# Second layer norm to first attention pair, reordered: token sums taken from PSUM, one gate chain for all tiles, odd value units and the first head's weights ahead of the experts

## What is computed

```
xn = layernorm(x)
x  = x + s4_convolution(xn) + swiglu_ffn(xn)
xn = layernorm(x)
x  = x + attention(xn) + lora_moe(xn)
```

## Time and profile before

| | |
|---|---|
| median of 3 runs | 1158.82 us (1155.83, 1158.82, 1159.38) |
| the profiled execution's own time | 1157.67 us |
| its span | 1155.8 us |
| TensorE busy | 1116.6 us, 97% of the span |
| VectorE, ScalarE, GpSimd busy | 680.5, 443.9, 741.8 us (59%, 38%, 64%) |
| TensorE's granted clock, mean | 0.988 of full speed |

### The profile page before, as it was taken

One profiled execution on the slowest core, in us unless ns is written; L12 is line 12 of the kernel. 1 busy time (PEld: TensorE's weight loads), 2 busy tenths in 40 slices (PEclk: granted clock), 3 DMA queues, 4 the chain that ended last, 5 costly groups with the idle time before them and its releaser, 6 DMA issues.

```text
span 1155.8 us, 19611 instructions
## 1 busy us (share of the span) xinstructions
PE 1116.6 (97%) x5822; PEld 956.6 (83%) x5822; DVE 680.5 (59%) x1673; ACT 443.9 (38%) x1287; POOL 741.8 (64%) x1107
## 2 busy tenths in 40 slices
PE   7989999986999999999999999999999999999997
PEld 7768888886788888888888888888888888888886
DVE  5777256287546546645664565466547645654575
ACT  2221132121344434444444444344434443444452
POOL 3654487767358766775876587667757766775552
PEclk8999999988999999999999999999999999999999
DMA  6212432111001101110111011002101110111001
GB/s 209 91 60 69 138 100 73 55 60 56 18 20 65 46 20 54 39 37 18 54 36 36 27 64 46 26 22 69 36 18 54 36 36 18 54 37 55 11 10 73
DMA packets 24825, 59.12 MB, mean 51 GB/s; under 512 B 3536, under 2 KB 3856, under 8 KB 24656
## 3 DMA queue, kind: packets, MB, share of 16 engines
q1 hardware_dynamic: 24784, 58.61, 15.5%
HBM read 56.50 MB, written 2.10 MB: 51 GB/s over the span
## 4 chain that ended last, share of the span: by engine, by line
PE 87%; DVE 7%; issue 2%; ACT 2%; POOL 1%; DMA 0%; SPq 0%; POOLq 0%; DVEq 0%; ACTq 0%
PE banks L169 26%; PE banks L171 26%; PE banks L170 26%; PE banks L1447 4%; PE banks L1438 2%; PE banks L1463 2%; DVE banks L1251 1%; POOL prob L1187 0%; PE banks L812 0%; ACT prob L1346 0%; DVE mixed L553 0%; ACT kT_hi L1229 0%; DMA acc<-in_x 0%; DVE prob L1368 0%; ACT oT_hi L1355 0%
## 5 line engine op out<-in xcount | busy, mean ns | idle before, releaser
L1186 POOL TENSOR_SCALAR prob<-prob,inv 128x128 f32<-128x128 f32 x128 | 48.0, 375 | 258.2 <-DVE inv L1374 258.2
L1159 POOL TENSOR_TENSOR form_lo<-wqk_stage,form_hi 128x256 fp32r<-128x256 f32 x192 | 142.0, 739 | 16.0
L1387 DVE TENSOR_TENSOR acc<-acc,banks 128x512 f32<-128x512 f32 x128 | 87.6, 685 | 81.1 <-PE banks L171 79.9
L1346 ACT ACTIVATE prob<-prob,top 128x128 f32<-128x128 f32 (+1 forms) x256 | 114.9, 452 | 34.9 <-DVE top L1368 34.5
L169 PE MATMUL banks<-tT_hi,form_hi 128*128 128x512 f32 x256 | 105.3, 411 | 0.0
L1368 DVE CUSTOM_DVE_ANT_0 prob<-banks,mask 128x128 f32<-128x128 f32 (+1 forms) x256 | 80.7, 353 | 40.2 <-PE banks L171 40.1
L171 PE MATMUL banks<-tT_hi,form_lo 128*128 128x512 f32 x256 | 100.2, 391 | 0.0
L169 PE MATMUL banks<-wv_hi,xT_hi 128*128 128x512 f32 x256 | 99.9, 390 | 0.0
L170 PE MATMUL banks<-tT_lo,form_hi 128*128 128x512 f32 x256 | 99.8, 390 | 0.0
L171 PE MATMUL banks<-wv_hi,xT_lo 128*128 128x512 f32 x256 | 99.6, 389 | 0.0
L170 PE MATMUL banks<-wv_lo,xT_hi 128*128 128x512 f32 x256 | 99.6, 389 | 0.0
(11 more groups left out here) (263 smaller groups left out, 3127.7 us busy)
## 6 DMA issues: line engine op xcount, KB each, us to landing
wqk_stage<-in_w_qk SPq DMA_DIRECT2D x32, 512.0 KB, 3.2
gu_stage<-in_w_gu SPq DMA_DIRECT2D x22, 512.0 KB, 3.3
wvo_stage<-in_w_v SPq DMA_DIRECT2D x32, 256.0 KB, 3.5
wvo_stage<-in_w_o SPq DMA_DIRECT2D x32, 256.0 KB, 2.6
wd_stage<-in_w_down SPq DMA_DIRECT2D x22, 256.0 KB, 2.6
acc<-in_x SPq DMA_DIRECT2D x8, 256.0 KB, 5.1
out<-acc SPq DMA_DIRECT2D x8, 256.0 KB, 2.0
tab<-in_w_comb SPq DMA_DIRECT2D x1, 1300.0 KB, 6.5
```

Source lines behind the costliest of these rows:

```text
L1159: nc.gpsimd.tensor_tensor(form_lo[:, part], src[:, :], as_f32(form_hi[:, part]), ALU.subtract).then_inc(form_ready, 1)
L1186: nc.gpsimd.tensor_scalar(prob[:, i, 0:P], prob[:, i, 0:P], inv[:, i, 0:1], 1.0, ALU.mult, ALU.mult)
L1346: ins = nc.scalar.activation(pr, pr, ACT.Exp, bias=top[:, n % 2, r:r + 1], scale=-1.0, accum_out=total[:, n % 2, r:r + 1])
L1387: nc.vector.tensor_tensor(acc[:, t, :], acc[:, t, :], turn_bank(steps, step), ALU.add).then_inc(w_added, 1)
```

## The change

The change edits only order, buffers and the way some sums are formed:

- **Token sums.** ScalarE copies only the first halves of the banks (256 of 512 columns) of tiles 0 to 3 and, new, those of tiles 4 to 7 (`b1`). A new VectorE step `keep(t)` takes one difference while tiles 0 to 3 are transposed. `mix(t)` becomes three instructions: two of 256 columns with one operand in PSUM and one of 512 columns with both in SBUF. Before it had two with a PSUM operand and two with none, of 256 columns each. The features of `tT` stand in another order, and P4 is combined with a subtraction.
- **Gates.** One chain for all eight tiles, behind `linear_add(7)`; the exponential's table is loaded ahead by a small activation behind `hg_copy(3)`. `hg`, `hw`, `ge`, `gw` and `gt` hold all tiles.
- **Value units 1, 3, 5, 7** of group 0 go ahead of P1, P6 and the gated transposes; the rest of head 0's ahead steps are spread finer. The first five slots lose these units.
- **GpSimd** makes all seven forms of head 0 between its two blocks of bias adds, behind a wait on the last down projection, and splits the four value pieces between `tT_lo` of tile 1 and of tile 2. The first two query and key loads wait for the last gate and up products and no longer for the end of the convolution; for this `wqk_stage` and the `late` buffers lie elsewhere.
- **Experts** use two banks (5 and 7) and no longer three; the wait for the last expert add moves to S of pair 1.
- In `OUTER_SLOTS` unit `("W", 1, 5)` and product `("P", 3, P4)` change places, and in the last group the pieces `WO[2:4]` are split at pair 13 and no longer at pair 14.

```diff
+AHEAD_V = 1, 3, 5, 7
 FIRST_SLOTS = [
-    [("L", 0, P5), ("V", 0), ("Y", 0), ("V", 1), ("P", 0, P3), ("P", 1, P1)],
-    [("L", 0, P3), ("P", 1, P6), ("V", 2), ("Y", 2), ("P", 1, P2), ("V", 3)],
-    [("L", 1, P2), ("P", 1, P7), ("V", 4), ("Y", 4), ("P", 1, P4), ("V", 5)],
-    [("L", 1, P4), ("P", 1, P5), ("V", 6), ("Y", 6)],
-    [("L", 1, P5), ("V", 7), ("P", 1, P3)]]
+    [("L", 0, P5), ("V", 0), ("Y", 0), ("P", 0, P3)],
+    [("L", 0, P3), ("V", 2), ("P", 1, P1), ("Y", 2), ("P", 1, P6)],
+    [("P", 1, P2), ("L", 1, P2), ("P", 1, P7), ("P", 1, P4)],
+    [("L", 1, P4), ("V", 4), ("Y", 4), ("P", 1, P5)],
+    [("L", 1, P5), ("V", 6), ("Y", 6), ("P", 1, P3)]]
...
-LAST_SPLITS = [[task for task in slot if task[0] != "wv" and (task[0] == "wo" or task[1] < GH)] for slot in SPLITS]
+LAST_SPLITS = [[task for task in slot if task[0] not in ("wv", "wo") and task[1] < GH] for slot in SPLITS]
+LAST_SPLITS[5], LAST_SPLITS[13] = WO[0:2], WO[2:4]
...
     def expert_bank(n):
-        return D + 1 + n % 3
+        return D + 1 + 2 * (n % 2)
...
             if t == TH:
+                pool.wait_ge(wd_used, 2 * NF)
                 ahead(0)
...
         for t in range(TH):
+            if t == 2:
+                ahead(1)
...
-        ahead(1)
...
         for t in range(TH):
             act.wait_ge(xT_done, NT + t + 1)
-            nc.scalar.activation(xh[:, t, :], banks[:, G + t, :], ACT.Copy).then_inc(xh_done, 1)
+            nc.scalar.activation(xh[:, t, 2 * P:], banks[:, G + t, 0:2 * P], ACT.Copy)
             xT_evac(NT + t, G + t)
         sqrt_var(4)
         hg_copy(range(0, 2))
-        for t in range(TH, NT):
-            xT_evac(NT + t, D + t - TH)
-        for t in range(2):
+        for t in range(TH):
+            act.wait_ge(xT_done, NT + TH + t + 1)
+            nc.scalar.activation(b1[:, t, :], banks[:, D + t, 0:2 * P], ACT.Copy)
+            xT_evac(NT + TH + t, D + t)
+        for t in range(TH):
             mixed_evac(t)
-        hg_copy(range(2, 3))
-        for t in range(2, TH):
-            mixed_evac(t)
-        hg_copy(range(3, TH))
-        gate_exps(0)
+            if t % 2:
+                hg_copy(range(2 + t // 2, 3 + t // 2))
+        nc.scalar.activation(gt[:, 9, :], gt[:, 8, :], ACT.Exp)
         hg_copy(range(TH, NT))
-        gate_exps(1)
+        gate_exps()
         ahead(0)
         hwT_evac(0)
+        ahead(1)
         hwT_evac(1)
-        ahead(1)
+        ahead(2)
...
+        def keep(t):
+
+            nc.vector.tensor_tensor(xh[:, t, 0:2 * P], xh[:, t, 2 * P:], banks[:, G + t, 2 * P:],
+                                    ALU.subtract).then_inc(x_kept, 1)
...
-            link(nc.vector.tensor_tensor(t1, b1, a1, ALU.subtract))
-            link(nc.vector.tensor_tensor(t2, b2, t1, ALU.subtract))
-            nc.vector.tensor_tensor(t3, t2, a1, ALU.subtract)
-            nc.vector.tensor_tensor(t4, a2, t2, ALU.subtract).then_inc(x_mixed, 1)
+            nc.vector.tensor_tensor(t1, wide(banks[:, D + t, 0:2 * P], 2), wide(xh[:, t, 2 * P:], 2), ALU.subtract)
+            link(nc.vector.tensor_tensor(t3, wide(banks[:, D + t, 2 * P:], 2), wide(b1[:, t, :], 2), ALU.subtract))
+            dve.wait_ge(x_kept, t + 1)
+            nc.vector.tensor_tensor(two.rearrange("p (f k) n -> p f (k n)", f=2), wide(xh[:, t, :], 2),
+                                    t3.rearrange("p k n -> p (k n)").unsqueeze(1).broadcast_to([P, 2, 2 * P]),
+                                    ALU.add).then_inc(x_mixed, 1)
...
-        gates(0)
         for n in range(TH, NT):
             linear_add(n)
-        gates(1)
+        gates()
+        ahead(0)
         hwT_evac(0)
-        ahead(0)
+        ahead(1)
         experts_add(0)
+        ahead(2)
         hwT_evac(1)
-        ahead(1)
+        ahead(3)
         experts_add(1)
-        ahead(2)
...
         pe.wait_ge(base_added, NT - 2)
         ahead(0)
+        pe.wait_ge(base_added, NT)
+        ahead(1)
         gated_transposes(0)
-        ahead(1)
+        ahead(2)
         experts(0)
+        ahead(3)
         gated_transposes(1)
-        ahead(2)
+        ahead(4)
         experts(1)
-        ahead(3)
-        pe.wait_ge(moe_added, NT)
...
         sp.wait_ge(credit_given, 1)
-        sp.wait_ge(y_done, NT)
+        sp.wait_ge(gu_used, 2 * NF + 2)
...
     def tensor_ahead(pe, part):
         if part == 0:
-            product(pe, 0, 0, P1, turn_bank(FIRST, ("P", 0, P7)))
+            pe.wait_ge(vo_ready, KD)
+            for n in AHEAD_V[0:2]:
+                values(pe, 0, FIRST, n)
             return
         if part == 1:
+            for n in AHEAD_V[2:4]:
+                values(pe, 0, FIRST, n)
             pe.wait_ge(mixed_ready, TH)
-        for i in (None, (P6,), (P2, P7), (P4, P5))[part]:
+        for i in (None, (P1, P6), (P2, P7), (P4,), (P5,))[part]:
...
     def gpsimd_ahead(pool, part):
         if part == 0:
-            for what in HEAD_BEGIN:
+            for what in HEAD_BEGIN + HEAD_END:
                 prepare(pool, 0, 0, what)
             return
-        for what in HEAD_END:
-            prepare(pool, 0, 0, what)
         for k in range(KD):
...
     def scalar_ahead(act, part):
         if part == 0:
-            copy_p1(act, 0, 0, turn_bank(FIRST, ("P", 0, P7)))
-            return
-        for i in (P2, P4, P5):
-            qk_evac_hi(act, 0, FIRST, 0, i)
+            for n in AHEAD_V:
+                values_evac(act, 0, FIRST, n)
+            copy_p1(act, 0, 0, turn_bank(FIRST, ("P", 0, P1)))
+        elif part == 1:
+            qk_evac_hi(act, 0, FIRST, 0, P2)
+        else:
+            qk_evac_hi(act, 0, FIRST, 0, P4)
+            qk_evac_hi(act, 0, FIRST, 0, P5)
...
                     if b % 2 == 0:
                         pe.wait_ge(mix_done, mixes(g, h, C12_LO if b else C21_LO))
+                    if n == 1 and steps is FIRST:
+                        pe.wait_ge(moe_added, NT)
```

More of the change, by code:

```diff
@@ L129, in turns @@
     else:
-        before = [("P", 0, P6), ("P", 0, P7)] if steps is FIRST else [("V", n) for n in (1, 2, 3)]
+        before = [("V", n) for n in (1, 2, 3)]
+        if steps is FIRST:
+            before = [("V", n) for n in AHEAD_V] + [("P", 0, i) for i in (P1, P6, P7)]
     return len(before), before + [s for s in steps if s[0] in "PVW" and is_long(s) == long]
@@ L186, in layer0 @@
     (hT_hi, hT_lo, gu_stage, gu_hi, gu_lo, wd_stage, wd_hi, wd_lo, work, toep_hi, toep_lo, tab) = ffn_sb
[L187 removed]
+    wc_hi, wc_lo, wb_hi, wb_lo, s4, hwT_hi, hwT_lo = expert_sb
     vcs, bps, sm, ex, exi, bb, vv, omc, cs, A, dsk, st, mv, ln, gt = small_sb
[L189 removed]
+    mixed, tT_hi, tT_lo, b1, mixed_ready = mix_sb
     xh = gu_stage.rearrange("p a b k n -> p (a b) (k n)")
@@ L407, in hg_copy @@
         def hg_copy(tiles):
[L408 to L413, removed]
+            for t in tiles:
+                act.wait_ge(base_done, t + 1)
+                nc.scalar.activation(hg[:, t, :], banks[:, linear_bank(t) + 1, DM - CUT:WC - CUT],
                                      ACT.Copy).then_inc(hg_done, 1)
@@ L736, in gates @@
             link(nc.vector.tensor_tensor(gw, gw, wide(9), ALU.mult))
[L737 to L743, removed]
+            for half in range(2):
+                ts = slice(half * TH, half * TH + TH)
+                nc.vector.tensor_tensor(hw[:, ts, :].rearrange("p t (e r) -> p t e r", e=NE),
+                                        hg[:, ts, 0:ER].rearrange("p t (e r) -> p t e r", e=NE),
+                                        gw[:, ts, :].unsqueeze(3).broadcast_to([P, TH, NE, RANK]),
+                                        ALU.mult).then_inc(hw_done, 1)
         def hwT_evac(half):
@@ L784, in vector_program @@
             xT_evac(NT + t, G + t)
+            keep(t)
         residual(1)
@@ L873, in gated_transposes @@
             pe.wait_ge(hw_done, half + 1)
-            pe.wait_ge(*((hwT_lo_done, 1) if half else (base_added, NT - 1)))
+            pe.wait_ge(hwT_lo_done if half else base_added, 1 if half else NT)
             for t in range(TH):
-                ins = nc.tensor.transpose(banks[:, D, t * P:(t + 1) * P], hw[:, t, :], ident[:, :])
+                ins = nc.tensor.transpose(banks[:, D, t * P:(t + 1) * P], hw[:, half * TH + t, :], ident[:, :])
             ins.then_inc(hwT_done, 1)
@@ L1259, in product @@
     def product(pe, g, h, i, bank):
-        right, k0, half = {P1: ((xT_hi, xT_lo), 0, 0), P6: ((tT_hi, tT_lo), 0, 0), P2: ((xT_hi, xT_lo), FT, 0),
-                           P7: ((tT_hi, tT_lo), FT, 0), P4: ((tT_hi, tT_lo), 2 * FT, 0),
+        right, k0, half = {P1: ((xT_hi, xT_lo), 0, 0), P6: ((tT_hi, tT_lo), FT, 0), P2: ((xT_hi, xT_lo), FT, 0),
+                           P7: ((tT_hi, tT_lo), 2 * FT, 0), P4: ((tT_hi, tT_lo), 0, 0),
                            P5: ((tT_hi, tT_lo), 3 * FT, 0), P3: ((xT_hi, xT_lo), FT, 1)}[i]
@@ L1288, in wait_turn, with values, values_evac @@
             pe.wait_ge(mix_done, mixes(g, older[1], freed))
+    def values(pe, g, steps, n):
```

(31 more changed lines are left out.)

97 lines of the change are left out of this document (43 added, 54 removed).

## The result

| | before | after |
|---|---|---|
| median of the runs | 1159.10 us (4 runs, 1155.83 to 1160.36) | 1139.03 us (4 runs, 1136.44 to 1139.96) |
| the profiled execution: own time, span | 1157.67, 1155.8 us | 1136.44, 1134.6 us |
| TensorE busy, mean granted clock | 1116.6 us, 0.988 | 1110.3 us, 0.994 |

The ratio is 0.983, with a 95% interval of 0.9811 to 0.9848: faster by 20.1 us.

The account below looks back on a forecast made before the run. TensorE, busy 97% of the span, was taken as the bound, with idle time and clock to win. 11.0 us of work done earlier and 2.5 in the tail take 13.5 off 1157.67, giving 1144.2; stated as 1144.5 us, range 1137.5 to 1151.5.

Parts of the forecast that it names:

- `linear(4)` and `linear(5)`: TensorE's waits for base adds: 0.5 us idle for 4.02, then 4.8 us idle and a slow spell of 2.3 us.
- The gates: One chain from near 273, 5.5 to 9 us, covered by TensorE's 13.8 us of work; the 6.92 us wait goes.
- The experts: Combines ahead of expert adds on VectorE cost 0.9 us in the first half and 1.4 in the second.
- The norm: VectorE's small operations for tiles 4 to 7 meet a busy GpSimd: 0.8 us in all, which TensorE can hide.
- rival C: Norm: GpSimd blocks each of five small VectorE operations, 4 us, 2.8 of it coming through: 1147.5 us; chance 0.1.
- GpSimd: Head 0's forms from 229.9 to 242.8, value pieces to 262, tT_lo to 267: all this costs nothing.
- The first slots: Slots lose 11 us of TensorE work; GpSimd's 5 to 7 us a slot still fits: 0 lost, bound +3.
- Rival D: First slots: T of pairs 0 to 4 waits 1 to 2 us each for GpSimd's probabilities, +7: 1151 us; chance 0.1.
- The swap: W(1,5) and P4 in the six middle groups: no more than 1 us either way, taken as 0.
- The tail: Last output weights split a pair earlier: gain 2.5 us, with TensorE's transposes 0.4 us later.
- rival B: GpSimd's gaps let VectorE through; wait ahead of linear(5) under 2.4 us, clock doesn't fall: 1139 us; chance 0.15.
- Rival E: Gap ahead of linear(5) drops the clock to 1.2 GHz, short waits keep it there: 1162 us, slower; chance 0.05.

Follow-up runs that it names:

- experiment 3: The kernel after, with WO[2:4] split at pair 14 again: 1142.79 us, ratio 0.9865.
- experiment 1: The kernel after, with W(1,5) back ahead of P(3,P4): 1143.20 us, ratio 0.988.
- Experiment 7: The kernel after, with tile 3's copies and linear_add(3) right behind those of tile 2, ahead of mix(2) and mix(3): 1134.29 us, ratio 0.978.
- Experiment 4: The kernel after, with all eight value units back in the first slots and none ahead: 1142.49 us, ratio 0.9872.
- Experiment 8: As Experiment 7, with the combines of P7 and P5 behind the expert adds: 1132.69 us, ratio 0.9774.
- experiment 2: The kernel before, with only the exchange of W(1,5) and P(3,P4): 1154.24 us, ratio 0.9967.
- experiment 5: The kernel after, with the 512-column sum of mix as two of 256 columns: 1139.19 us, ratio 0.9831.
- experiment 9: As Experiment 8, with the late forms of experiment 6: 1136.34 us, ratio 0.9814.
- experiment 6: The kernel after, with head 0's last five forms back behind tT_lo of tile 1, ahead of the value pieces: 1136.71 us, ratio 0.981.

## Why the prediction was right, and where it was not

**`linear(4)` and `linear(5)`: right in place, a little too dear.** Forecast were 0.5 and 4.8 us idle and 2.3 of slow matmuls, 7.6 in all; measured 0.69, 3.69 and 1.5, 5.9. The chain was the one described: `mix(3)`'s long sum ended at 254.4, VectorE's add at 256.4, and `linear(5)` began 15.7 us after `linear(2)` where the working had 16.4. The slow spell is the term that varies: behind a wait of 3.7 us `linear(5)` lost 1.5 us here and in experiment 3, and the forecast 2.3 in experiments 1 and 4. One block a tile was right: the four long sums took 1.09 to 1.80 for the 0.68 that I read without a block, so 0.4 to 1.1 each, mean 0.8 for the forecast 0.7. Experiment 7 shows that the wait was the order of VectorE's and ScalarE's queues and no need of the data.

**The gates: right.** The chain ran from 270.17 to 275.33, 5.2 us with GpSimd idle, just under the 5.5 to 9 of the forecast, and the value units hid it. Experiment 4 shows that without them 2.57 of it and 1.32 at a base add come back.

**The experts: too dear.** 0.41 and 0.90 for 0.9 and 1.4. Experiment 8 took both away by the two combines that the prediction had named.

**The norm: right, rival C fell.** VectorE's small operations between 234 and 237 us took up to 0.4 above their usual 0.2, about 0.8 in all; the two worst:

```profile
235.66 0.33 DVE L503 TENSOR_TENSOR ln<-ln 128x4 f32<-128x4 f32 x1
...
236.22 0.59 DVE L505 TENSOR_TENSOR ln<-ln 128x4 f32<-128x4 f32 x1
```

TensorE was busy without a break from 228 to 241 us.

**GpSimd: right.** The seven forms ran from 228.23 to 240.8, the value pieces to 261.1, `tT_lo` to 265.9, and then, behind two steps of head 1's first form, it was idle for 14.53 us until P1's product.

**The stretch: 57.6 us forecast from `linear(2)` to S of pair 0, 55.75 measured.** The two items above saved 1.7 and 1.0; the work at full clock took 0.9 more than I had summed, 48.6 for 47.7.

**The first slots: 0 forecast, 0.7 lost.** Rival D was there in miniature, with another wait than I named: not GpSimd's probabilities but `v_lo`. O of pair 2 starts on TensorE at 319.21, just behind VectorE's remainder of value unit 4:

```profile
318.42 0.69 DVE L1414 TENSOR_TENSOR v_lo<-banks,v_hi 128x512 fp32r<-128x512 f32 x1 [0.32 <-ACT v_hi L1320]
```

**The swap: the term that failed.** "The waits in the six middle groups are too small for more than 1 us either way; I take 0." It gave 5.2 us, and experiments 1 and 2 show that it was the swap. The seven waits in question (the six middle groups and the first) are listed with 2.8 us in all; by the starts of the scores they cost 4.4, some 0.2 more each, and smaller steps of some 0.14 a group make up the rest. I had also not asked what stands behind P4's evacuation in ScalarE's queue.

**The tail: right.** 2.3 us for 2.5. The four steps now stand a pair earlier:

```profile
1113.92 1.29 POOL L1177 TENSOR_TENSOR tT_lo<-wvo_stage,tT_hi 128x512 fp32r<-128x512 f32 x1
1115.19 0.38 POOL L1196 TENSOR_SCALAR prob<-prob,inv 128x128 f32<-128x128 f32 x1
```

and the price, transposes late by 0.4, was 0.19 by the list and 0.35 by the starts (0.47 behind the matmul ahead of them for 0.12), with 0.20 more listed at W(2, 0).

**The sum.** Forecast 13.5. Measured on the spans: 1.7 in the stretch, 11.0 of units gone, -0.7 in the first slots, 5.2 from the swap, 2.3 in the tail, and 1.8 that the start of this execution gave, 21.3 for 21.2. Without the 1.8 it is 19.5, and the medians say 20.1. Most of the difference between forecast and result is the swap, and most of the rest the stretch. The forecast itself holds a slip: 1144.2 and the 1.15 by which the median stood above the profiled execution make 1145.3, not 1144.5. That the median fell inside the range is partly luck: without a price for the swap it came to lie 1.5 us above the lower bound, and that bound was set by rival B. Rival B named 1139, which is what came, but not for its reason: the wait ahead of `linear(5)` was there and the clock fell behind it. Rival E fell too; the clock was back by 261.

## What to carry to other kernels

Price a reordering in the steady part of a kernel by how often it recurs, and a short wait by starts and not by the listed idle time: 0.33 us listed was 0.55 lost, and seven of them a fifth of the gain between the two traces. For a swap, look at every in-order queue that takes the result and ask what stands behind it there. Where an engine waits long, ask first whether the instruction that releases it could stand earlier in its queue: moving one add with its copies (experiment 7) took 3.69 us of idle time off, where making the sums ahead of it 2.8 us longer (experiment 5) cost 1.3 us in the trace and nothing that the medians show.

## What the runs showed of the hardware

**The same idle time, two prices.** Ahead of `linear(5)` TensorE was idle for 3.69 us in the kernel after and 3.70 in experiment 1. The table of stages after shows a granted clock of 0.86 and 0.97 for 250 to 270 us; in experiment 1 it is

```profile
250.00:260.00 10.00, 6.30 (x31) 6.11 (x31) 6.00 (x11) 3.96 (x6) 8.94 (x9) 0.75 0.35 111
260.00:270.00 10.00, 10.00 (x64) 10.00 (x64) 1.50 (x4) 0.57 (x2) 7.13 (x5) 0.90 0.16 49
```

Slice by slice the clock was at the lower level for some 3.4 us in the one, from 257.2 on, and for 6.8 in the other, from 255.1 on. `linear(5)` took 5.2 us in the one and 6.0 in the other, for 3.7 at full clock. The tail of the kernel before and that of experiment 2 are the same code with the same wait, 2.96 us in both. Before, no slow matmul followed, and the last scores began 21.75 us ahead of the end. In experiment 2 the third matmul behind the wait has 0.63, the clock was at 0.50 from 1133 to 1136, and it is 23.2 us:

```profile
1132.32 0.47 PE L169 MATMUL banks<-tT_hi,wv_hi 128*128 128x512 f32 x1 [2.96 <-POOL tT_lo L1165]
```

An idle time of 3.11 (experiment 9) was followed by no slow matmul, one of 2.95 (experiment 3) by the longest slow spell in a tail. So what a wait of about 3 us costs beyond itself is a spread, from nothing to some 2.6 us (experiment 3), and a single execution does not tell it.

**A block ends with GpSimd's instruction.** An operation of VectorE on 256 columns with both operands in SBUF, 0.42 us alone, took up to 2.55 beside GpSimd in experiment 5; one of twice the size, 0.69 alone, took 1.1 to 1.8 in the kernel after and 2.82 in experiment 6. In the cases that I read, the held operation ended 0.27 us (256 columns) or 0.55 (512) after GpSimd's current one: 249.57 after 249.30, 249.40 after 248.85. So a block costs what is left of GpSimd's instruction, once for each of VectorE's that meets one, and not by the column.
